# Expert numbers loaded four at a time, and the end of the second attention reordered, in a two-attention, two-router kernel on one core

## The reference, cut to what matters

```
x = x + attn_a(layernorm(x))     # windowed attention and MLP
x = x + ffn(layernorm(x))        # 8 experts, the 2 best per token
x = x + attn_b(layernorm(x))     # 7 windows of 128 per batch, halves overlap
x = x + ffn(layernorm(x))        # the same experts again

def ffn(x, W1, W2, Wr):
    logits = einsum('btd,ed->bte', x, Wr)
    probs  = softmax(logits)
    topk_vals, topk_idx = top_k(probs, 2)
    gate   = router weights at the two chosen experts, 0 elsewhere
    h = silu(einsum('btd,efd->btef', x, W1))     # 128 -> 512
    y = einsum('btef,edf->bted', h, W2)          # 512 -> 128
    return einsum('bte,bted->btd', gate, y)
```

## Time and profile before

| | |
|---|---|
| median of 3 runs | 565.09 us (564.62 to 568.42) |
| the profiled execution, its own time | 566.33 us |
| its span, first to last instruction | 564.5 us |
| mean granted TensorE clock | 0.934 of full speed |
| PE busy | 488.1 us, 86% of the span |
| DVE, ACT, POOL busy | 292.4, 250.6 and 247.5 us |
| first and second stage of experts on PE | 267.8 to 366.6 and 450.0 to 546.6 us |

### The profile page before, as it was taken

The page is one execution under the profiler, slowest core; times in us unless marked ns, Lnnn a source line. Parts: engine busy times, 40 slices in busy tenths (PEclk is TensorE's granted clock), DMA queues, the critical chain, the costliest instruction groups (busy, mean ns, idle before and its releaser), DMA issues.

```text
span 564.5 us, 12563 instructions
## 1 busy us (share of the span) xinstructions
PE 488.1 (86%) x4071; PEld 378.0 (67%) x4071; DVE 292.4 (52%) x960; ACT 250.6 (44%) x529; POOL 247.5 (44%) x229
## 2 busy tenths in 40 slices
PE   1989999999999999899979999937998499999970
PEld 0647776868666887766867787715777297787750
DVE  5556495948796789746731010057577743010115
ACT  7754566573645444333322323346663122232333
POOL 7134262435332464641676253621146567343460
PEclk9998898999898999989889999969998679999995
DMA  7865292967396337011132310040001223311007
GB/s 234 255 145 82 61 171 63 171 135 104 86 148 134 66 95 130 15 34 39 39 87 82 82 35 24 36 149 2 1 19 40 66 68 82 86 53 35 21 30 224
DMA packets 66594, 48.36 MB, mean 86 GB/s; under 512 B 7861, under 2 KB 60615, under 8 KB 66534
## 3 DMA queue, kind: packets, MB, share of 16 engines
q1 hardware_dynamic: 61430, 36.99, 30.8%
q0 software_dynamic: 5104, 10.57, 5.3%
HBM read 16.14 MB, written 27.59 MB: 77 GB/s over the span
## 4 chain that ended last, share of the span: by engine, by line
PE 70%; DVE 11%; issue 6%; DMA 5%; POOL 3%; SPq 2%; ACT 2%; POOLq 0%; DVEq 0%; ACTq 0%
PE PS L817 14%; PE PS L658 9%; PE PS L801 7%; PE PS L803 4%; PE PS L645 3%; PE PS L710 3%; PE PS L620 3%; PE PS L802 3%; PE PS L639 3%; PE PS L556 2%; DMA X<-in_x 2%; PE PS L602 2%; PE PS L668 2%; PE PS L629 2%; SPq L303 2%
## 5 line engine op out<-in xcount | busy, mean ns | idle before, releaser
L507 POOL DMA_INDIRECT YY<-W2R,ID x78 | 77.0, 988 | 81.4 <-ACT W2R L1296 62.8
L451 POOL TENSOR_TENSOR R<-NM,I64B 128x1024 bf16<-128x1024 f32 x32 | 61.4, 1920 | 114.0 <-DVE NM L1464 109.0
L1288 ACT ACTIVATE W2R<-PS 128x512 f32<-128x512 f32 x78 | 46.6, 597 | 125.9 <-PE PS L803 125.8
L817 PE MATMUL PS<-WB,W2R 128*128 x624 | 90.5, 291 | 0.0
L495 POOL DMA_INDIRECT XS<-W1R,SLOT x64 | 64.0, 1000 | 48.0 <-DVE SLOT L1590 31.4
L801 PE MATMUL PS<-QKM,WA 128*128 128x128 bf16 x312 | 71.7, 232 | 9.6 <-issue 4.4
L817 PEld LDWEIGHTS PS<-WB,W2R 128*128 128x128 f32 x624 | 77.8, 197 | 2.4 <-issue 0.2
L1741 DVE COPY QKM<-PS 128x1024 bf16<-128x1024 bf16 (+1 forms) x20 | 13.5, 677 | 123.6 <-PE PS L780 123.6
L803 PE MATMUL PS<-QKM,WA 128*128 128x128 bf16 x312 | 71.7, 232 | 0.0
L802 PE MATMUL PS<-QKM,WA 128*128 128x128 bf16 x312 | 69.5, 225 | 0.0
L658 PEld LDWEIGHTS PS<-VB,PF 128*128 128x128 f32 x512 | 60.1, 193 | 9.2 <-issue 9.2
(11 more groups left out here) (207 smaller groups left out, 871.2 us busy)
## 6 DMA issues: line engine op xcount, KB each, us to landing
XS<-CST SPq DMA_DIRECT2D x30, 520.0 KB, 9.9
QKM<-XS SPq DMA_DIRECT2D x78, 65.0 KB
QKM<-QK SPq DMA_DIRECT2D x64, 72.0 KB, 2.1
QKM<-YY SPq DMA_DIRECT2D x16, 256.0 KB, 4.8
W2R<-in_W POOLq DMA_DIRECT2D x1, 2048.0 KB, 12.3
YY<-W2R,ID POOLq DMA_INDIRECT x78, 2.2
XS<-CST SPq DMA_DIRECT2D x2, 585.0 KB, 9.0
XS<-W1R,SLOT POOLq DMA_INDIRECT x64
```

Source lines behind the costliest of these rows:

```text
L451: nc.gpsimd.tensor_tensor(R[:, u % 2], NM[:, u % 2].unsqueeze(2).to_broadcast([P, NH, WIN]), I64B[:].unsqueeze(1).to_broadcast([P, NH, WIN ...
L507: pool.indirect_dma_start(out=YY[f], out_offset=to, in_=YS[n % NY][:, i, :], in_offset=None, bounds_check=NPAIRS - 1, oob_is_err=False) \
L817: last = mm(o, HF[n % 3][:, k, :], WB[:, e, k, :].rearrange("p o c -> p (o c)"), start=k == 0, stop=k == KF - 1)
L1288: fn(HF[n % 3], PS[:, n % 3, :].rearrange("p (k s) -> p k s", k=KF), ACT.Silu).then_inc(s["f_hf"], 1)
```

## The change

Three things are edited.

1. `choose` takes a group instead of a tile: one TENSOR_LOAD fills the registers of up to four tiles, and the bounds' arithmetic and assertion are left out. It stands behind `turned` of the group and ahead of `outputs` (behind it where a new phase opens).
2. In the second attention's end, batch 1's `route_x_t` stands ahead of `b_weighted(2)` on PE and of `b_context(2)` on ACT, its `logits` ahead of `b_scores(3)`, its `route_choose` ahead of `b_max(3)` on DVE and its `ranks` ahead of `b_values(3)`. `b_output(2)` and its variance come ahead of `b_divide(3)`, `route_table(1, 0)` and `route_choose(1, 2)` ahead of `b_output(3)`. POOL sends the first row block of batch 0 ahead of batch 1's `rstd` instead of the first two, and the first two of batch 2 ahead of batch 3's.
3. Batch 3's routing moves into the expert loop: `ROUTED[1]` becomes (0, 1, 3), its normalisation stands behind `turned(0)` on DVE. Six `keep_busy` matmuls that waited for batch 3's `rstd` become twice fourteen that wait for nothing, on both sides of batch 2's `ranks`.

```diff
@@ POOL @@
-            dispatch(1, 0, range(2))
+            dispatch(1, 0, range(1))
             rstd(0, "f", B + 2, o=NT + TB)
-            dispatch(1, 0, range(2, 8))
-            dispatch(1, 1, range(2))
+            dispatch(1, 0, range(1, 8))
+            dispatch(1, 1, range(3))
             rstd(0, "f", B + 3, o=NT + TB)
-            dispatch(1, 1, range(2, 8))
+            dispatch(1, 1, range(3, 8))
+            dispatch(1, 2, range(2))
             rstd(0, "f", 2 * B, o=NT + TB)
-            dispatch(1, 2)
+            dispatch(1, 2, range(2, 8))
@@ PE @@
-        ROUTED = ((3, 4, 6), (-1, 0, 2))
+        ROUTED = ((3, 4, 6), (0, 1, 3))
-                def choose(t):
+                def choose(g):
+                    tiles = GROUPS[g]
                     for i, (_, t0, _) in enumerate(PHASES):
-                        if t == t0:
+                        if tiles[0] == t0:
                             pe.wait_ge(s["f_table"], 2 * (NPH * f + i + 1))
-                    which[t] = pe.value_load(EID[0:1, t:t + 1], min_val=0, max_val=NE - 1)
+                    _, experts_of = nc.values_load_multi_w_load_instructions(
+                        EID[0:1, tiles[0]:tiles[-1] + 1], engines=[mybir.EngineType.PE], min_val=0, max_val=NE - 1,
+                        skip_runtime_bounds_check_because="a count of at most NE experts, clamped to 1 and less 1")
+                    which.update(zip(tiles, experts_of))
@@ the loop @@
-                else:
-                    route_x_t(f, B - 1)
                 for t in range(NTILE + 2):
                     if t < NTILE:
                         hidden(t)
                     late = t // 4 * 4 + 4 in [t0 for _, t0, _ in PHASES]
                     if t < NTILE and t % 4 == 2 + late and t // 4 + 1 < NGRP:
                         turned(t // 4 + 1)
+                        if not late:
+                            choose(t // 4 + 1)
                     if t >= 2:
                         outputs(t - 2)
-                    if t + 1 < NTILE:
-                        choose(t + 1)
+                    if t < NTILE and t % 4 == 3 and late:
+                        choose(t // 4 + 1)
                     routed(t)
@@ PE, second attention @@
+                if b == B - 2:
+                    route_x_t(1, b - 1)
                 b_weighted(b)
-                if b:
+                if b in (1, B - 1):
                     route_x_t(1, b - 1)
+                if b == B - 2:
+                    logits(1, b - 1)
                 if b < B - 1:
                     b_scores(b + 1)
-                if 1 <= b < B - 1:
+                if b == 1:
                     logits(1, b - 1)
                 b_output(b)
                 if b == B - 1:
                     logits(1, b - 1)
+                    keep_busy(0, 14)
+                if b >= B - 2:
+                    ranks(1, b - 1)
                 if b < B - 1:
                     b_values(b + 1)
+                if b == 1:
+                    ranks(1, b - 1)
                 if b == B - 1:
-                    pe.wait_ge(s["f_rstd"], 2 * B)
-                    keep_busy(0, 6)
-                if b:
-                    ranks(1, b - 1)
+                    keep_busy(0, 14)
@@ DVE, experts(1) @@
                     turned(0)
                     identities(0)
+                    route_normalised(f, c)
+                    route_split(f, c)
                     route_choose(f, c)
-                    route_table(f, 1)
-                    route_place(f, c)
                     turned(1)
                     identities(1)
+                    route_place(f, c)
+                    route_table(f, 1)
@@ DVE, second attention @@
+                if b == 2:
+                    route_choose(1, 1)
                 b_max(b + 1)
-                if b:
-                    route_choose(1, b - 1)
+                if b == 1:
+                    route_choose(1, 0)
...
-            b_divide(B - 1)
             b_output(B - 2)
             b_variance_out(B - 2)
+            b_divide(B - 1)
             route_normalised(1, B - 2)
             route_split(1, B - 2)
+            route_table(1, 0)
+            route_choose(1, B - 2)
             b_output(B - 1)
-            route_table(1, 0)
+            route_place(1, B - 2)
             b_variance_out(B - 1)
-            route_choose(1, B - 2)
-            route_place(1, B - 2)
-            route_normalised(1, B - 1)
-            route_split(1, B - 1)
```

More of the change, by code:

```diff
@@ L1297, in y_out @@
                         .then_inc(s["f_ys"], 1)
-                if f:
-                    route_x_t(f, B - 1)
                 for t in range(NTILE):
```

## The result

| | before | after |
|---|---|---|
| median of the runs | 564.86 us (4 runs, 561.84 to 568.42) | 531.68 us (4 runs, 529.14 to 545.12) |
| profiled execution | 566.33 us, span 564.5, mean clock 0.934 | 532.24 us, span 530.4, mean clock 0.934 |
| ratio | | 0.9395, 95% interval 0.9319 to 0.9472 |

The account below looks back on a forecast made before the run. PE's queue, not its array, was taken to set the pace at 2.25 us a tile. Gains of 17.5 + 17.7 + 2.1 - 0.5 = 36.8 us from 565.09 gave 528 us, with 518 to 540 as the range.

Parts of the forecast that it names:

- First stage: 17.5 us less 0.5: First expert stage, `outputs(6)` to its end: 74.5 us shrink to the array's 55.0, less 2.0 for unevenness; 17.5 us gained.
- I take off **0.5 us: First stage, third phase's gate: `turned(4)` reached near 304 us, batch 3's rows landing between 303.4 and 305.4; 0.5 us lost.
- Second stage: 17.7 us: Second stage from `turned(2)`: 77.7 us against the array's 57.2, less 1.2 for unevenness and 1.6 for half clock.
- left for one load of four numbers: PE's queue in a group: array needs 7.0 us, leaving 0.75 us free; load put in lower half of 0.30 to 1.2.
- unevenness: Deductions from the loads' gain: 2.0 us in the first stage, 1.2 in the second, there including a wait for a copy.
- Head and gate: 2.6 us sooner at `hidden(0)`, 2.1 at `turned(2)`: Second stage's start: `hidden(0)` near 447.4 us instead of 449.99, `turned(2)` at 466.8 instead of 468.88; only 2.1 us counted.
- PE is busy from 431.4 us on without a break by this order, so I take full clock: Ahead of the second stage: fillers take 6.4 us at full clock instead of 12.8, ending with `ranks` at 446.0 us.
- doesn't bound: POOL's indirect DMAs in the expert stages: 1.26 us each, one a tile, under 1.75 us, so no limit.
- That only the gap closes: Rival on PE's queue: each tile saves only 0.33 us, stages gain 10 + 10 us, 543 us; 12 in 100.
- That four numbers cost four loads: Rival on PE's queue: a load of four takes 1.3 us, costing 10 us over 15 groups, 538 us; 15 in 100.
- The fillers as bound: Rival ahead of the second stage: fillers at half clock delay `hidden(0)` 4 us and the queue gains nothing, 569 us; 2 in 100.
- That the reordering alone fails: Rival at the second stage's gate: phase 1's table 3 to 5 us later, loss up to 3, 531 to 533 us; 15 in 100.

Follow-up runs that it names:

- loads only: Kernel before with only the grouped, unchecked load of expert numbers at the group's place, old order kept; ratio 0.9422 to before, 528.6 us.
- the order alone: Changed kernel with the old load, one number a tile with arithmetic and assertion, at its old place; ratio 1.0022 to before, 562.3 us.
- table early: Changed kernel with the second stage's table for tiles 8 to 15 ahead of batch 3's choice, behind batch 2's placing; ratio 0.9328 to before, 525.1 us.
- no fillers: Changed kernel without its 28 `keep_busy` fillers ahead of the second stage; ratio 0.9444 to before, 531.7 us.
- load twice: Changed kernel with each group's four numbers loaded twice, one register set for `hidden`, one for `outputs`; ratio 0.9471 to before, 537.1 us.
- four loads: Changed kernel with four loads of four numbers in each group, each tile using one number of its own load; ratio 0.9658 to before, 548.5 us.
- the rows first: Changed kernel, first stage: POOL sends batch 3's rows ahead of the first outputs, batch 3's `ranks` one tile sooner; ratio 0.9353 to before, 530.3 us.
- table between: Changed kernel with batch 3's rows first and the second stage's table between batch 3's split and choice; ratio 0.9298 to before, 526.0 us.
- pairs from tile 24 on: The kernel with rows first and table between, with output rows of tiles 24 to 31 sent in pairs; ratio 0.9253 to before, 523.5 us.
- both: Changed kernel with batch 3's rows first in the first stage and the table early in the second; ratio 0.9315 to before, 524.2 us.

## Why the prediction was right

**What bounds the kernel.** Right: the gain is the queue's, the loads alone give it, and the order alone gives nothing. `hidden` takes the 0.67 us forecast, a group 7.30 us where 7.0 to 7.3 were.

**First stage: 17.5 us less 0.5.** Measured 12.1 us behind `turned(2)`, 4.9 short. The step that failed is "I take off **0.5 us**" for the third phase's gate. It was reached some 4 us ahead of its rows, and what came behind ran at half clock for a while. I had timed batch 3's rows by those of before; but they stand in POOL's order behind outputs that PE makes, and a dip of its clock ahead of these delays them. The runs with the same POOL order and tiles nearly as fast part in two. With a dip ahead of POOL's first output block (after, 0.57 in its worst 5 us; table early, 0.63) POOL idles 4.80 and 4.78 us ahead of that block and `turned(4)` waits 3.95 and 4.36 us. Without one (loads only, no fillers, load twice, four loads; "no fillers" dips at 280 to 286 us, behind its first block at 277.56) POOL idles 1.68 to 1.69 us and the wait is 0.87, 1.16, 1.36 and 1.35 us. With the rows first it is none, with the dip ("table between") and without it, and the stage gives the whole: 78.3 to 60.9, 17.5 us. So 0.5 us was too little even without the dip, where the wait is some 1.2 us, and that the dip fell there in the profiled run was bad luck.

**Second stage: 17.7 us.** Measured 16.6, with the half clock behind `turned(2)` as foreseen; 17.0 where that wait was taken away.

**The load of four.** Its length, 0.33 us, is close to the lower bound, 0.30 us. The 0.75 us "left for one load of four numbers" are not: a second load adds 0.43 us to each group. That the error made little difference to the time is luck: what one load costs on the path was in part set aside as unevenness (2.0 + 1.2 us in 15 groups are 0.21 each; measured are 7.30 - 7.0 = 0.30). The Trainium skill's floor of some 600 ns for a register load (DMA: Bandwidth & Descriptors, "Latency and other measured facts") is not borne out: the instruction takes 332 ns, all that belongs to it some 400. The 200 ns for each register that the Trainium skill gives (Runtime: NRT & Kernel Launch, "Instruction fetch mechanics"), on a page that speaks of loads from HBM, don't carry over to this load from SBUF: three more numbers cost 30 ns.

**Head and gate: 2.6 us sooner at `hidden(0)`, 2.1 at `turned(2)`.** Mis-sized: the head gained 1.6 us over eight runs, and 0.4 in the profile of after. The step that was off is "PE is busy from 431.4 us on without a break by this order, so I take full clock". The busy stretch begins 66.1 us behind the first stage's end, where 431.4 us would be 64.8: ahead of it PE waits 3.29 us for batch 3's softmax, 2.03 before (3.28 or 3.29 in every run with the new order). And the weighted sums in it still run at half clock, 3.36 us, where batch 2's take 1.73. So the fillers begin at 75.5 us and not at 73.0. PE waits at `turned(2)` as forecast, 5.3 us for 4. But the table for tiles 8 to 15 is ready 94.1 us behind the stage's end and not 92.7, so of the 2.1 us only 0.3 came. The loads alone gain 1.9 us at this gate, since PE came to it late before and it had nearly opened; on top of them the new order adds nothing, as its table stands behind batch 3's choice.

**The tail: nothing forecast, 1.0 us lost.** That POOL, with 1.26 us for an indirect DMA against 1.75 us a tile, "doesn't bound" holds for the mean, but fails at the stage's end: POOL's last block follows PE's last `outputs` by 2.97 us instead of 2.07 in the first stage, and in the second the last transfer starts 2.9 us behind it instead of 2.1. I had put this down to the outputs coming in fours; pairs from tile 24 on took back 0.13 us of it in the first stage, so why POOL falls behind stays open.

**The rivals.** That only the gap closes is out (`hidden` 0.67 us). That four numbers cost four loads is out for the numbers; four instructions do cost more, and more than it priced: 8.46 us a group and 548 us, for its 538. The fillers as bound: hardly. `turned(0)` starts right behind them and without a wait (429.87 us), and without them `hidden(0)` starts 0.5 us sooner, which is less than runs differ. That the reordering alone fails, losing what the gate gives, was nearest: its mechanism, a later table, is what was found, at 1.4 us rather than 3 to 5. With 5.0 us of clock in favour of the profile of after and 4.9 us short in the first stage, two misses of opposite sign made the profiled time come out close: that is luck. Without the first stretch the two profiles lie 29.1 us apart where 36.8 was forecast; the profiled time would have been 537 us, near the upper end of the range. The medians, 33.2 us apart, share the clock's luck less.

## What to carry to other kernels

Where a tensor engine's matmuls are addressed by registers, read its queue beside its array: time without anything to wait for ahead of weight loads is the sign, and the cost goes by the number of load instructions and by what the compiler adds to each (bounds arithmetic, assertion), so load many numbers at once. Spare time of a queue that is spread over many instructions is not to be booked against a new one in a lump; put a second one in and see. When a stage becomes a fifth faster, list every gate inside it and what stands ahead of each in the program of the engine that opens it: here PE waited 9.2 us at two gates of the profiled run, some 2.7 us of it for a dip of the clock, and moving eight DMAs, a set of ranks and one table opened both, without any work added or removed.

## What the runs showed of the hardware

- A load of four numbers into registers took 0.332 us in PE's queue, of one number 0.302 us (medians of 20 and 78). On the path a load more cost 0.38 us (one number, spread), 0.39 (four numbers, bunched) and 0.43 us (a second one of four) in a group.
- Arithmetic (0.151 us) and assertion (0.018 us) on a loaded number, 0.17 us by their own rows, cost 0.29 us each on the path. What the other 0.12 us are, no view shows.
- By the prediction's count PE's queue needs 1.45 us for a tile without its load and the array 1.62, and a load of 0.33 us still showed as 0.26 us more in the two `outputs` behind it. How far the queue is or can be ahead of the array wasn't measured.
- The kernel before was granted mean clocks between 0.926 and 0.949 over its executions, and the dips moved from profile to profile. Five us between two profiles of nearly the same order go with it: "both" has 520.0 us at 0.949, "table between" 524.8 at 0.936, though its expert stages and gate sum to 1.1 us less (219.1 for 220.2).
